# x by tokens loaded behind the spectral blocks, copies moved in the opening chunks, a smaller taps operation, four more groups to GpSimd

## The reference, cut to what matters

```python
x = x + _L0_conv_ref(_ln_c(x), L0_conv_kernel_base)
t = _to_tokens(x)
t = t + _L0_ffn_ref(_ln_t(t), router_w, router_b, expert_w, expert_b)
x = _from_tokens(t, x)
x = x + _L1_conv_ref(_ln_c(x), L1_conv_kernels)
t = _to_tokens(x)
t = t + _L1_ffn_ref(_ln_t(t), router_w, router_b, expert_w, expert_b)
```

## Time and profile before

| | |
|---|---|
| Runs | 957.55 us median of 3 (956.13 to 961.07) |
| Profiled execution, its own time | 955.84 us |
| Span of its instructions | 954.1 us |
| Busy share of the span | PE 89%, PEld 73%, DVE 81%, ACT 53%, POOL 59% |
| Mean granted TensorE clock | 0.936 of full speed |
| Spectral layer | 0 to 187 us of the span |
| Experts of layer 0 | 187 to about 480 us |
| Depthwise convolution | about 480 to 690 us |
| Experts of layer 1 | about 690 to 954 us |

### The profile page before, as it was taken

How to read it: one execution, slowest core, us unless ns; L and a number is a source line. 1 busy time by engine, 2 the same in 40 slices (tenths; PEclk the granted TensorE clock), 3 DMA queues, 4 the chain that set the end, 5 groups by cost and what they waited for, 6 DMA issues and landing times.

```text
span 954.1 us, 24392 instructions
## 1 busy us (share of the span) xinstructions
PE 850.6 (89%) x9482; PEld 699.1 (73%) x9482; DVE 774.4 (81%) x1421; ACT 506.9 (53%) x1051; POOL 567.5 (59%) x504
## 2 busy tenths in 40 slices
PE   6997888677999998996899999999658999999998
PEld 6996877645676666654899999999635666667665
DVE  5768698888999989999787677774787999998884
ACT  2467485786667766211444444444168676676511
POOL 3780203157798887796654334330216888889888
PEclk9997577988999999999899999999959999999999
DMA  9997100103777776683787877888000010101101
GB/s 377 355 294 258 50 1 2 40 15 153 281 311 300 301 300 274 280 323 122 265 282 253 286 264 259 274 275 264 13 1 13 33 46 24 45 24 45 46 40 49
DMA packets 48291, 163.09 MB, mean 171 GB/s; under 512 B 9424, under 2 KB 9936, under 8 KB 46032
## 3 DMA queue, kind: packets, MB, share of 16 engines
q1 hardware_dynamic: 48208, 161.96, 46.7%
HBM read 93.46 MB, written 68.49 MB: 170 GB/s over the span
## 4 chain that ended last, share of the span: by engine, by line
PE 50%; DVE 31%; POOL 6%; issue 5%; DMA 3%; ACT 3%; SPq 1%; POOLq 0%; DVEq 0%; ACTq 0%
PE pair L1692 23%; DVE R L904 11%; PE pair L1619 5%; PE pair L1605 5%; PE pair L1606 4%; DMA X<-x_rows 3%; PE pair L1616 3%; DVE R L844 3%; PE pair L1492 3%; POOL R L571 3%; DVE R L660 2%; PE pair L1583 2%; DVE R L833 2%; DVE work L660 2%; ACT pair L1249 1%
## 5 line engine op out<-in xcount | busy, mean ns | idle before, releaser
L904 DVE TENSOR_TENSOR R<-pair,R 128x896 f32<-128x896 f32 x256 | 275.1, 1082 | 41.8 <-PE pair L1606 40.6
L571 POOL TENSOR_TENSOR R<-R 128x768 f32<-128x768 f32 x128 | 231.9, 1812 | 85.8 <-DVE R L904 76.7
L1692 PE MATMUL pair<-R 128*128 (+4 forms) x2880 | 226.8, 242 | 9.8 <-DVE R L982 9.2
L1692 PEld LDWEIGHTS pair<-R 128*128 128x128 f16 x2880 | 223.9, 98 | 12.9 <-issue 10.5
L1249 ACT ACTIVATE pair<-X,work 128x64 f32<-128x64 f32 x480 | 166.7, 394 | 97.1 <-DVE R L844 94.6
L1605 PE MATMUL pair<-work,R 128*128 128x448 f16 x512 | 185.0, 361 | 22.4 <-DVE R L904 20.9
L1606 PE MATMUL pair<-work,R 128*128 128x448 f16 x512 | 184.4, 360 | 0.0
L581 POOL TENSOR_TENSOR R<-R 128x512 f32<-128x512 f32 x128 | 164.9, 1288 | 10.0
L997 DVE COPY R<-R 128x1152 f32<-128x1152 f32 x64 | 93.1, 1455 | 64.9 <-PE pair L1692 64.3
L1367 ACT COPY R<-R 128x1152 f32<-128x1152 f32 x64 | 81.9, 1282 | 117.4 <-PE pair L1692 117.4
L1619 PE MATMUL pair<-R,ident_sb 128*128 128x256 f32 x496 | 128.4, 381 | 0.0
(11 more groups left out here) (137 smaller groups left out, 1292.7 us busy)
## 6 DMA issues: line engine op xcount, KB each, us to landing
taps_halves<-R SPq DMA_DIRECT2D x128, 458.5 KB, 3.3
R<-taps_halves SPq DMA_DIRECT2D x64, 917.0 KB, 4.8
X<-x_tok SPq DMA_DIRECT2D x4, 2048.0 KB, 17.8
out<-X SPq DMA_DIRECT2D x15, 512.0 KB, 2.6
R<-spec_pairs SPq DMA_DIRECT2D x16, 272.0 KB, 5.4
X<-x_rows SPq DMA_DIRECT2D x4, 1024.0 KB, 10.6
R<-x_chan SPq DMA_DIRECT2D x4, 1024.0 KB, 13.7
X<-x_rows SPq DMA_DIRECT2D x2, 2048.0 KB, 27.3
```

Of the source, the lines that this page charges most:

```text
L571: pool.tensor_tensor(pr[:, :, 192:384], pr[:, :, 0:192], pr[:, :, 192:384], ALU.add).then_inc(half_ready, 1)
L904: dve.tensor_tensor(pr.rearrange("p t (e c) -> p t e c", c=C), pair[p % 2][:, :].rearrange("p (t e c) -> p t e c", t=2, c=C)[:, :, 0:NE - ...
L1692: mm = pe.matmul(acc[:, y0:y1, x0:x1, :], blocks[i % 2][:, ks, 2 - y, 1 - x, :], src[:, y0 + y:y1 + y, x0 + x:x1 + x, :], start=(ks == 0 a ...
```

## The change

Four edits. POOLED grows from four groups to eight. The four DMAs of x by tokens move from behind the blocks of step 2 to behind the blocks of all steps and the expert weights. DVE's low part of the taps takes the 29 by 29 region in place of the whole row. In `start_chunk`, of both layers, the order within a pair changes: second half of a normalisation, then copies, then the first half of the next normalisation; at the pairs 3 and 5 the copies thereby come ahead of the first half.

```diff
-        POOLED = (2, 5, 8, 11)
+        POOLED = (2, 5, 8, 11, 15, 18, 21, 24)
...
                 for r in BLOCKS:
                     sp.dma_start(k_raw[t % 3][r], spec_pairs[:, PER_STEP * t:PER_STEP * t + PER_STEP, :]
                                  ).then_inc(k_in[t % 3], 16)
-                if t == 2:
-
-                    sp.wait_ge(piece_measured, len(UNITS))
-                    for i in range(4):
-                        n = NT * C // 4
-                        sp.dma_start(X[:, i * n:(i + 1) * n], x_tok[:, i * n:(i + 1) * n]).then_inc(x_in, 16)

             wait_c_dft_low(sp, 32)
             sp.dma_start(raws_at[0], experts0).then_inc(raw_in, 16)
+            sp.wait_ge(piece_measured, len(UNITS))
+            for i in range(4):
+                n = NT * C // 4
+                sp.dma_start(X[:, i * n:(i + 1) * n], x_tok[:, i * n:(i + 1) * n]).then_inc(x_in, 16)
...
-                dve.scalar_tensor_tensor(out=taps_16[r], in0=taps_f32[r], scalar=TAP_SCALE, in1=taps_16[r],
+                first = CENTRE - KS // 2 * (PITCH + 1)
+                f32, f16_ = (m[r, first:first + KS * PITCH].rearrange("p (x y) -> p x y", y=PITCH)[:, :, 0:KS]
+                             for m in (taps_f32, taps_16))
+                dve.scalar_tensor_tensor(out=f16_, in0=f32, scalar=TAP_SCALE, in1=f16_,
                                          op0=ALU.mult, op1=ALU.subtract).then_inc(taps_step, 1)
...
                 for p in range(NPAIR):
                     if p % 4 == COPY_AT and p >= 4 * SUM_LAG:
                         copy_sum(layer, 0, p // 4 - SUM_LAG)
-                    if p in START_NORMS:
-                        k, j = START_NORMS[p]
-                        normalise(layer, k, k % 2, j, range(0, 4))
                     if p - 1 in START_NORMS:
                         k, j = START_NORMS[p - 1]
                         normalise(layer, k, k % 2, j, range(4, 8))
                     if p in START_TURNS:
                         k, j = START_TURNS[p]
                         copy_parts(layer, k, k % 2, j)
+                    if p in START_NORMS:
+                        k, j = START_NORMS[p]
+                        normalise(layer, k, k % 2, j, range(0, 4))
```

## The result

The changed kernel takes 961.11 us (median of 20 runs, 960.01 to 962.24), the kernel before 957.33 us (20 runs); the ratio is 1.0037, 95% interval 1.0028 to 1.0045. I had forecast 952.7 us in a range up to 959.5. The result lies 1.6 us above that range; against the kernel before it is 0.37% slower, less than the half per cent that I had called no change. The profiled execution's span grew from 954.1 to 958.9 us.

What follows compares the result with a forecast made beforehand. Bound: a relay between PE and DVE. Sum +1.25 - 0.5 - 4.0 - 1.6 = -4.85 us; against the median of 957.55 forecast as 952.7 us, range 946.5 to 959.5.

Steps and rivals of the forecast that it cites:

- x by tokens moved: Mode mixing: first code gap shrinks, three later packet ends come under the load; +1.25 us, ends -2.35 and +6.2.
- The price of a packet end under x by tokens: End of the mode mixing: each new packet end under the load costs 1.2 us, between nothing and 2.85; +3.6 us together.
- The number of packet ends: Mode mixing: three packet ends, after 655, 783 and 911 matmuls, now lie under x by tokens.
- The gain at the first gap: Start of the mode mixing: PE's first issue gap falls from 2.85 to about 0.5 us, -2.35 us.
- Rival 1: Mode mixing: code packets wait for a whole transfer of x, 5.2 us, at three ends; 964.7 us; chance 0.12.
- Rival 2: Mode mixing: code does not feel x by tokens at all; -2.35 for that edit, 949.1 us; chance 0.20.
- Four more groups to POOL: Inverse groups: DVE loses four additions, POOL gains them, ACT gains four copies; -0.5 us, ends -2.4 and +2.0.
- Rival 3: Inverse groups: ACT becomes the bound, +2.0 in place of -0.5 us, 955.2 us; chance 0.13.
- Copies ahead of normalisations: First chunks of both layers: PE's turn starts earlier as ACT copies first; -1.8 and -2.2 us, together -4.0.
- what is late next is DVE itself: Layer 0's first chunk: after the earlier copies DVE has no idle left to the taps; gain taken as 1.8 us.
- Rival 4: First chunks: reordering does not do what it says, DVE held elsewhere; -0.8 in place of -4.0, 955.9 us; chance 0.10.
- The taps: Low part of the taps: DVE's operation shrinks from 2412 to 841 elements, ending 0.88 us behind POOL's addition; -1.6 us.

Runs made afterwards that it cites:

- the shifted code: Changed kernel with 64 more long-met waits written on PE ahead of the mixing's row transforms (32 more instructions in the trace); 956.24 us, a single run.
- the kernel with the load alone: Kernel before with only x by tokens moved behind the blocks and the expert weights; 965.44 us, ratio 1.0078.
- the filled pause: Changed kernel with x by tokens in its old place, plus 26 unread PE transposes where PE waits at layer 1's chunk 1; 951.83 us, ratio 0.9932.

## Why the prediction was wrong, and where it was right

**x by tokens moved: forecast +1.25 us, measured +8.62.** This term alone carries the miss. Three of its steps failed, and the kind of cost was right: the "issue" gaps are ends of packets of code, as the shifted code and the packets' own records showed, and the load of x lengthens them.

- *The price of a packet end under x by tokens.* I took 1.2 us, between 0.70 and 2.85, and chose the end near 0.70 as its DMA share was the same. It was 3.45, 2.14, 2.13 and 2.35 us. The share of busy time was the wrong likeness: 0.91 beside the blocks and 0.96 to 0.99 beside x look alike, and the ends cost three to five times as much. The rate differs (271 GB/s against 393 to 410), but it is no sure measure either: the end of 2.85 us stood beside 211 GB/s. That row was of the right size, and partly by luck: the trace of before has the last row of x by tokens at 83.66 us and this packet of code only at 86.49, so most of its wait was beside blocks. No row of before had a packet end under x by tokens alone.
- *The number of packet ends.* I counted three, behind 655, 783 and 911 matmuls, and let the one behind 527 stay at 0.70. It lay under x by tokens too and was the dearest. Four ends cost 10.07 us; at 1.2 us each for three I had 3.6.
- *The gain at the first gap.* It fell from 2.85 to 1.12 us in the changed kernel, and the first three together from 3.47 to 2.00, which looks like a good part of my 2.35. But with the load behind the mixing altogether the sum is 5.07 us, not 4.17 - 2.35. What the first end gains, the later ones lose to the blocks.

The arithmetic closes: the gaps grew by 12.07 - 4.17 = 7.90 us, and the trains of matmuls themselves by 0.71 (28.78 us in sum against 28.07), which makes 8.61, the table's 8.62 but for rounding.

Rival 1 had the sign, and its point of decision (2.8 us a packet, for three) was nearly met by 2.5 us for four. Its mechanism, one whole transfer of 5.2 us, was not what happened: no gap reached that, and pieces of a quarter of the size changed nothing. A chance of 0.12 was too little for it, as I had let the mechanism stand for the cost. Rival 2, no effect of x on the code, is refuted by the kernel with the load alone.

**Four more groups to POOL: forecast -0.5, measured -0.3** in the trace. Kernels with eight groups have that stretch 0.3 us shorter than those with four at a like clock, which is less than the times can show. The steps are there to be seen: the fills at the place worked out, the fourth low part (191.02) at once behind ACT's cast (which ends at 190.97). Rival 3, ACT as the bound there, did not come.

**Copies ahead of normalisations: forecast -1.8 and -2.2; measured -1.2 in layer 0, -1.6 and then -0.1 in layer 1.** The mechanism was right: PE's waits fell by 1.5 us, where 1.4 was forecast, and the 2.13 us went. In layer 0 the sentence "what is late next is DVE itself" failed: ACT was late next. From 205.75 on it works without a pause, and its copy of the sum comes only 1.1 us earlier than before, counted from pair 0, where the pairs come 1.6 us earlier; PE waits 0.83 us for it. So the 0.70 us of DVE's wait at pair 10, which was to go, became 1.18, and the gain lies near the lower end of my 1.0 to 1.85. In layer 1 the same wait for ACT came (0.82 us), and the 1.5 us that were lost at the beginning of chunk 1 go with the clock, as the filled pause showed; they are not the order's own price, as 1.2 of them were lost with the old order too. I had written that the clock might hide or double a microsecond, but behind the mixing; I did not look for pauses behind which it could fall. Rival 4 did not hold in layer 0, and in layer 1 not for the reason that it gave.

**The taps: forecast -1.6, measured -1.65.** The end 0.90 us behind POOL's addition is what the share of the elements gave (0.88). The rule of the Trainium skill, "SBUF — State Buffer", section "SBUF: two separate sides", fits the trace from both sides here: DVE behind POOL, and then POOL's addition of 1.94 us behind DVE.

**The sum.** -4.85 forecast, +4.83 in the trace: of the 9.7 us between them 7.4 are the load's, 2.1 layer 1's, 0.6 layer 0's copies and 0.2 the groups', less 0.4 that the changed kernel gained between the taps and layer 1 and 0.2 at the mixing's start and in the taps.

Two figures beside the forecast were also off. Its chances give "faster" 0.46, but half of 0.45 and all of 0.20 make 0.43 at most. Its lower bound of 946.5 does not come out of what it names: rival 2's 949.1 with the copies at 4.68 and the taps at 2.3 is 947.7. Neither touches the miss, which lay at the other end.

Two things stay open. A packet of code under a full load is late because it begins late; what holds its beginning up is narrowed (not the size of the transfers, and less with one small piece at a time, as if it waited behind what is queued) but not settled. And why the clock falls behind one pause and not behind its like in the kernel before is not shown by any run; only that filling the pause keeps it up.

## What to carry to other kernels

A load that no reader waits for is not free while an engine runs short instructions in long straight code: the code itself comes by DMA, so put large loads where the busy engine uses its code slowly. Price a collision by a row with the same load beside it, not by one with the same busy share, and where there is no such row, let the range reach the worst row in sight. Look at the packets of the code queue by themselves: they say when a fetch began and ended. Before counting a shortened wait as gained, look for the next pause of PE on the way: of 1.6 us won by ACT's copies in layer 1, 1.5 were lost behind the next pause, at the lower clock. Split an edit on the chip: its sum can hide more than it tells, as here, where three parts gain 4.5 us and the fourth loses 7.

## What the runs showed of the hardware that was not expected

- PE at 27.8 ns a matmul uses up 16 KB of code (128 matmuls with their weight loads) in 3.56 us, and here it was fetched hardly faster: with the DMA engines idle a packet began about 1 us after PE had gone on with the one before, took 0.93 us, and elsewhere PE went on about 1.4 us behind a packet's end, some 3.3 us in all. Even then some ends waited for 0.15 to 0.22 us. Under x by tokens at about 400 GB/s packets began 3.4 to 4.6 us after, and the ends waited for 2.1 to 3.5 us. The Trainium skill, "Runtime: NRT & Kernel Launch", section "Instruction fetch mechanics", has lines of 16 KiB fetched ahead in sequence, with which the packets of the earlier trace rows agree (0.90 MB in 55). It also says that this fetch is hidden by the pace of dispatch, and here the measurement differs, by 12.07 us in one stage.
- In a single run, 32 more instructions ahead of a stretch, waits that were long met, moved its stalls and took 3.7 us out of the gaps (12.07 to 8.41).
- Transposes whose result nobody uses saved 1.5 us in each of the two layers, as the clock behind them stayed at 1.00 in place of 0.50 to 0.82.
